# A graph layer with a routed expert layer on one core: another order for the first loads, for TensorE's last products of a step, and for GpSimd's tail

## The chip, the cores and the metric

The program runs on one core of a Trainium2 chip. The metric is the device time of one execution in microseconds. TensorE does matrix products and transposes, VectorE (DVE in the profile), ScalarE (ACT) and GpSimd (POOL) the rest, and SyncE (SP) issues most loads. Each engine runs its own list of instructions in order; they meet at semaphores.

## The reference

`x` has 32 x 256 tokens of 128 values, `adj` 32 matrices of 256 x 256.

```python
def gnn(x, adjacency, epsilon, W1, b1, rms_weight, W2, b2):
    agg = epsilon * x + einsum('bnm,bmd->bnd', adjacency, x)
    h = einsum('bnd,dh->bnh', agg, W1) + b1                  # 128 -> 512
    h = silu(h * rsqrt(mean(h * h) + 1e-6) * rms_weight)
    return einsum('bnh,hd->bnd', h, W2) + b2                 # 512 -> 128

def ffn(x, gamma, beta, Wr, br, W1, b1, W2, b2):
    xn = layernorm(x) * gamma + beta
    top2 = top_k(xn @ Wr + br, 2)                            # of 8 experts
    return sum over the two of softmax_share * (gelu(xn @ W1[e] + b1[e]) @ W2[e] + b2[e])

x = x + gnn(layernorm(x), adj, ...)
x = x + ffn(layernorm(x), ...)
```

## The kernel before

**First part.** The 8192 tokens are 16 groups of 512 (4 tiles of 128 tokens). `STEPS` is 19, and a step works on up to six groups at once, each at another stage: group s is loaded and normalised (`stats1`, `add_epsilon`, `normalise1`), group s-1 is aggregated over its neighbours (`aggregate`), group s-2 is widened to 512 (`widen`, `square`, `weigh`, `rms`), group s-3 gets its silu, is transposed and narrowed (`silu`, `turn_hidden`, `keep_turned`, `narrow`), group s-4 is added to its input, normalised, transposed and sent through the router (`residual`, `stats2`, `scale2`, `normalise2`, `turn_to_features`, `expert_input`, `router`), group s-5 gets its two experts, its shares and its places (`route`, `shares`, `choose`, `rank_pairs`, `places`), and the rows of group s-6 are stored into a table in DRAM (`rows_dram`), sorted by the pair of experts (`send_rows`, one indirect DMA of GpSimd for each tile). Each engine's order within a step is written out by hand.

**Second part.** There are 28 pairs of experts. The second part takes 92 tiles of 128 rows of one pair each: 20 tiles (`EARLY`) that are known to be full after group 11, 44 more, and 28 partly filled ones. For tile i SyncE loads the rows (`load_rows`, into a ring of `RING` = 16 buffers; from tile 16 on it waits until the result of the tile 16 before has been stored). TensorE's step i transposes tile i, multiplies tile i-2 with the two experts' first weights (`w1_low`, `w1_high`), and tile i-4 with the second weights. For the first 64 tiles the first weights are copied to a fixed place, since they are known only at run time: both halves by ScalarE in tiles 0 to 19, and from tile 20 on the high half of every even tile by GpSimd (`place_high`). ScalarE applies gelu, VectorE adds biases and shares and writes `result` (12 buffers), and GpSimd stores it (`send_result`, an indirect DMA). VectorE's `tail` does the rest of groups 14 and 15 between the first 15 tiles, and so do the lists of the other engines, since the rows of the last groups must be stored before tile 20 can be loaded.

**GpSimd's tail before** is a list by hand: the four sends of group 13 in two pairs around `scale2` and `put_tokens` of group 15, `shares` of group 14, four sends of group 14, three results, `shares` of group 15, three results, four sends of group 15, nine results (6 to 14), and then one result for each step.

**The start.** SyncE loads `x_tok` of group 0 and at once `adj` of group 0. ScalarE's queue loads the constants (`fixed`, 207 KB), `eps_col`, then `gw1_sb`, `gb1_row` and `rms_bc`, which share the semaphore `wide_in`. TensorE's list begins with `sum_weights`, which waits for all three, and only then comes `aggregate(0)`. `fold_gw1` on VectorE adds the sums to the weights, and `widen(0, 0)` waits for that.

## Time and profile before

| | |
|---|---|
| median of 3 runs | 462.79 us (462.18 to 462.91) |
| profiled execution, its own time | 462.02 us |
| its span, first to last instruction | 460.2 us |
| TensorE busy | 404.1 us (88%) |
| VectorE, ScalarE, GpSimd busy | 306.8, 280.3, 247.4 us |
| first part at a steady pace | 12.98 us a step |
| tile 20 to tile 91 in the second part | 1.9 to 3.3 us a tile |

A row of a timeline gives start and length in us, the engine, the line of the kernel, the operation with its tiles as out<-in, and in brackets how long the engine sat idle and what ended that. "issue" is time in which an engine waited for nothing that the profile shows, and "remote" (or "another core or an unknown queue") is a wait that the profile can put down to no finished instruction. PEclk is TensorE's granted clock, 1.0 being its higher level.

### The profile page before, as it was taken

Reading aid. Unit: us, or ns where it says so; the run is one execution under the profiler, and the core shown is the slowest. Engines: PE = TensorE matmul, PEld = TensorE weight load, DVE = VectorE, ACT = ScalarE, POOL = GpSimd, SP = SyncE. Lnnn points to the kernel's source line nnn. Section 1 sums busy time; section 2 is a strip of 40 time slices with the busy share of each in tenths; the row PEclk is TensorE's granted clock in tenths of the full one; section 3 lists DMA queues with packets and bytes.
Section 4 is the critical chain, followed back from the end, with each engine's and each line's share of the span. In section 5 each row is a group of like instructions: output and inputs, shape, how many; then the busy total and the mean of one; then the engine's idle time right before and its main releaser. Section 6 shows DMA issues by size and latency. Waiting matters only on the chain.

```text
span 460.2 us, 11870 instructions
## 1 busy us (share of the span) xinstructions
PE 404.1 (88%) x2894; PEld 346.2 (75%) x2894; DVE 306.8 (67%) x1303; ACT 280.3 (61%) x645; POOL 247.4 (54%) x315
## 2 busy tenths in 40 slices
PE   1999999999999999998739487999999999999970
PEld 0557877877777777776729486999999889999970
DVE  4596777889887777768544393666666766656540
ACT  1278776778777777787637253766666666444520
POOL 1123546676667777766642544465556555545450
PEclk9999999999999999999967887999999999999995
DMA  6679773223233221111253223555554433433110
GB/s 206 180 228 309 249 232 92 85 95 114 95 105 115 86 80 46 41 47 38 77 146 86 91 89 95 146 147 154 139 131 127 137 107 107 114 101 105 36 43 6
DMA packets 40890, 53.24 MB, mean 116 GB/s; under 512 B 5812, under 2 KB 35636, under 8 KB 40183
## 3 DMA queue, kind: packets, MB, share of 16 engines
q1 hardware_dynamic: 33040, 32.95, 25.9%
q0 software_dynamic: 6096, 18.52, 11.9%
q10 hardware_dynamic: 1686, 1.01, 0.8%
q8 instruction: 26, 0.43, 0.4%
q14 instruction: 42, 0.34, 0.3%
HBM read 37.75 MB, written 22.31 MB: 131 GB/s over the span
## 4 chain that ended last, share of the span: by engine, by line
PE 56%; DVE 11%; issue 10%; DVEq 9%; ACT 4%; another core or an unknown queue 3%; POOL 2%; DMA 2%; ACTq 0%; POOLq 0%
PE banks L576 10%; PE banks L599 9%; PE banks L737 9%; PE banks L724 9%; PE banks L564 6%; PE banks L585 5%; PE banks L621 3%; DVEq L1417 2%; DVEq L1434 2%; PE banks L611 2%; DVE acc L1417 2%; DMA rms_bc<-rms_w 2%; DVE result L1442 1%; DVEq L1442 1%
## 5 line engine op out<-in xcount | busy, mean ns | idle before, releaser
L526 POOL DMA_INDIRECT out<-result,rows_in x92 | 89.8, 976 | 81.9 <-DVE result L1442 68.1
L737 PE MATMUL banks<-w_sb,hidden_e 128*128 (+1 forms) x736 | 102.3, 283 | 4.8 <-DVE result L1442 2.5
L737 PEld LDWEIGHTS banks<-w_sb,hidden_e 128*128 128x128 f32 x736 | 92.5, 196 | 7.9 <-issue 7.3
L877 ACT ACTIVATE hidden_e<-banks 128x512 f32<-128x512 f32 x92 | 55.0, 598 | 56.3 <-PE banks L724 30.7
L489 POOL DMA_INDIRECT rows_dram<-rows_out,row_of x64 | 66.6, 1040 | 25.2 <-issue 14.7
L599 PE MATMUL banks<-gw_sb,hidden_t 128*128 128x128 f32 x512 | 68.8, 277 | 0.0
L576 PE MATMUL banks<-gw_sb,agg 128*128 128x512 f32 x128 | 66.3, 603 | 0.8 <-ACT agg L812 0.8
L599 PEld LDWEIGHTS banks<-gw_sb,hidden_t 128*128 128x128 f32 x512 | 63.5, 192 | 0.8
L1428 DVE SCALAR_TENSOR_TENSOR acc<-banks,rows_in,acc 128x128 f32<-128x128 f32 x92 | 32.2, 350 | 46.7 <-PE banks L737 25.0
L797 ACT ACTIVATE hidden<-hidden,rrms 128x512 f32<-128x512 f32 x64 | 45.7, 715 | 18.0 <-POOL rrms L466 18.0
L990 DVE TENSOR_TENSOR hidden<-banks,rms_bc 128x512 f32<-128x512 f32 x64 | 43.9, 687 | 12.2 <-ACT hidden L789 12.2
L871 ACT ACTIVATE xg_t<-banks,ones 128x128 f32<-128x128 f32 x92 | 33.5, 364 | 30.3 <-PE banks L706 14.6
L789 ACT ACTIVATE hidden<-banks 128x512 f32<-128x512 f32 x64 | 38.2, 597 | 22.0 <-PE banks L576 20.0
L585 PEld LDWEIGHTS banks<-fixed,hidden 128*128 128x128 f32 x256 | 30.1, 141 | 26.7 <-issue 22.3
L1417 DVE SCALAR_TENSOR_TENSOR acc<-b_bc,rows_in 128x128 f32<-128x128 f32 x92 | 33.4, 363 | 20.2 <-DVE result L1442 15.5
L724 PE MATMUL banks<-xg_t,w_low 128*128 128x128 f32 x256 | 41.9, 289 | 0.0
L724 PE MATMUL banks<-xg_t,w_high 128*128 128x128 f32 x256 | 41.3, 286 | 0.0
L585 PE MATMUL banks<-fixed,hidden 128*128 128x128 f32 x256 | 38.9, 275 | 2.7 <-ACT hidden_t L804 2.0
L706 PE MATMUL banks<-fixed,rows_in 128*128 128x128 f32 x92 | 26.4, 287 | 16.5 <-ACT xg_t L871 16.2
L804 ACT ACTIVATE hidden_t<-banks 128x512 f32<-128x512 f32 x64 | 37.8, 590 | 2.8 <-PE banks L585 2.6
L1434 DVE SCALAR_TENSOR_TENSOR acc<-b_bc,rows_in,acc 128x128 f32<-128x128 f32 x92 | 32.5, 353 | 10.1 <-issue 6.0
L453 POOL TENSOR_TENSOR rstd<-var,minus_half 128x4 f32<-128x4 f32 x16 | 16.6, 1039 | 41.5 <-DVE var L1017 41.5
(141 smaller groups left out, 708.1 us busy)
## 6 DMA issues: line engine op xcount, KB each, us to landing
rows_in<-rows_dram SPq DMA_DIRECT2D x92, 132.5 KB
adj<-adj_t SPq DMA_DIRECT2D x16, 512.0 KB, 3.9
x_tok<-x SPq DMA_DIRECT2D x16, 256.0 KB, 3.9
rows_dram<-idle_in POOLq DMA_DIRECT2D x1, 3710.0 KB
rows_dram<-idle_in SPq DMA_DIRECT2D x28, 132.5 KB
out<-result,rows_in POOLq DMA_INDIRECT x92
w_sb<-w SPq DMA_DIRECT2D x1, 1024.0 KB, 6.3
b_bc<-b SPq DMA_DIRECT2D x1, 1024.0 KB, 11.5
```

Source lines behind the costliest of these rows:

```text
L489: nc.gpsimd.indirect_dma_start(out=rows_dram, out_offset=bass.IndirectOffsetOnAxis(ap=row_of[:, g * TPG + t:g * TPG + t + 1], axis=0), in_ ...
L526: nc.gpsimd.indirect_dma_start(out=out, out_offset=bass.IndirectOffsetOnAxis(ap=rows_in[:, i % RING][:, IDX_AT:IDX_AT + 1].bitcast(U32), a ...
L576: pe.matmul(hid_ps[:, n % 3], agg[:, g % 2, t * P:(t + 1) * P], gw1_sb[:], start=True, stop=True).then_inc(hid_done, 1)
L585: last = pe.transpose(hidt_ps[:, c * P:(c + 1) * P], hidden[:, n % HR, c * P:(c + 1) * P], ident)
L599: last = pe.matmul(z_ps[:, t * P:(t + 1) * P], hidden_t[:, g % 2, c, t * P:(t + 1) * P], gw2_sb[:, c], start=False, stop=True, skip_group_ ...
L724: last = pe.matmul(h_ps(i)[:, w * HCE + c], w1_now[:, c * P:(c + 1) * P], xg_t[:, i % 4], start=True, stop=True)
L737: last = pe.matmul(y_ps(i)[:, w], hidden_e[:, i % 4, w * HCE + c], w2_sb[:, bass.ds(at + c * D, D)], start=(c == 0), stop=(c == HCE - 1))
L797: nc.scalar.activation(hidden[:, n % HR], hidden[:, n % HR], ACT.Silu, scale=rrms[:, g % 2, t:t + 1]).then_inc(silu_done, 1)
L877: nc.scalar.activation(hidden_e[:, i % 4], h_ps(i), ACT.Gelu).then_inc(gelu_done, 1)
L990: nc.vector.tensor_tensor(hidden[:, n % HR], hid_ps[:, n % 3], rms_bc[:], ALU.mult).then_inc(weighted, 1)
L1417: nc.vector.scalar_tensor_tensor(acc[:, i % AHEAD], b2_bc[:, bass.ds(expert(words, i, D, True), D)], rows[:, bass.ds(expert(words, i, 1, T ...
L1434: nc.vector.scalar_tensor_tensor(acc[:, i % AHEAD], b2_bc[:, bass.ds(expert(words, i, D, False), D)], rows[:, bass.ds(expert(words, i, 1, ...
```

## The change

- **First loads.** `fixed` is split: the identity (first 128 columns) is loaded first, the rest with the small loads. SyncE issues `adj` of group 0 only after `x_tok` of group 0 has landed, and ScalarE's queue waits for the same before `gw1` (now into `gw1_raw`, a slot of `hidden`), `gb1` spread over all partitions (`gb1_bc`, another slot) and `rms_bc`, with semaphores of their own.
- **The fold of gb1 into gw1.** `row_part` and its matrix product are gone. VectorE's `mix_gw1` makes gw1 + gb1/128 in step 0, `sum_weights` is one product of the raw weights and stands behind `aggregate(0)` in step 1, and `fold_gw1` moves to step 1. `prep_rank` moves to step 3.
- **Order within a step.** On TensorE `turn_to_features` moves behind `narrow(g3, 2)` and `router` behind `narrow(g3, 3)`; on ScalarE `keep_turned(g3, 3)` stands ahead of `expert_input(g4)`. On GpSimd `rms` works on two tiles at a time, twice a step, and the four sends of a group stand one by one between other work.
- **Second part.** `RING` is 20. GpSimd copies the high weights of all even tiles below 64, also of the first 20. Its tail is another list: the sends of rows and results stand between the copies, at most three or four in a row, results 0 to 3 in pairs. After the tail it is behind with the results (8 is the last sent), sends one result in each step from 20 to 22, and catches up in step 23.

```diff
-RING, SENDS = 16, 12
+RING, SENDS = 20, 12
...
         first_loads = [
-            (fixed[:], fixed_in), (eps_col[:], eps.partition_broadcast(P)),
-        ]
-        wide_loads = [
-            (gw1_sb[:], gw1), (gb1_row[:], gb1), (rms_bc[:], rms_w.partition_broadcast(P)),
+            (fixed[:, 0:P], fixed_in[:, 0:P]), (eps_col[:], eps.partition_broadcast(P)),
         ]
...
         def high_by_gpsimd(i):
-            return EARLY <= i < NT and i % 2 == 0
+            return i < NT and i % 2 == 0
...
+                if g == 0:
+                    sp.wait_ge(x_in[0], 16)
...
-            def rms(g):
-                pool.wait_ge(sumsq_ready, TPG * (g + 1))
+            def rms(g, half):
+                tiles = slice(2 * half, 2 * half + 2)
+                pool.wait_ge(sumsq_ready, TPG * g + 2 * half + 2)
...
                 if g6 is not None:
-                    send_rows(g6, (0,))
+                    send_rows(g6, 0)
+                if g4 is not None:
+                    put_tokens(g4)
+                if g6 is not None:
+                    send_rows(g6, 1)
                 if g4 is not None:
                     scale2(g4)
-                    put_tokens(g4)
...
-                    send_rows(g6, (1, 2, 3))
+                    send_rows(g6, 2)
                 if g2 is not None:
-                    rms(g2)
+                    rms(g2, 0)
+                if g6 is not None:
+                    send_rows(g6, 3)
+                if g2 is not None:
+                    rms(g2, 1)
...
-            send_rows(NG - 3, (0, 1))
+            send_rows(NG - 3, 0)
+            pool.wait_ge(table_ready, 2)
+            place_high(0)
+            send_rows(NG - 3, 1)
+            place_high(2)
+            send_rows(NG - 3, 2)
+            send_rows(NG - 3, 3)
             scale2(NG - 1)
             put_tokens(NG - 1)
-            send_rows(NG - 3, (2, 3))
             shares(NG - 2)
-            send_rows(NG - 2, (0, 1, 2, 3))
-            for i in range(3):
-                send_result(i)
-            shares(NG - 1)
-            for i in range(3, 6):
-                send_result(i)
-            send_rows(NG - 1, (0, 1, 2, 3))
-            for i in range(6, EARLY - SUM_LAG - 1):
-                send_result(i)
+            place_high(4)
+            send_rows(NG - 2, 0)
+            place_high(6)
+            send_rows(NG - 2, 1)
+            send_rows(NG - 2, 2)
+            send_rows(NG - 2, 3)
+            place_high(8)
+            send_result(0)
+            send_result(1)
+            shares(NG - 1)
+            place_high(10)
+            send_result(2)
+            send_result(3)
+            place_high(12)
+            send_rows(NG - 1, 0)
+            place_high(14)
+            send_rows(NG - 1, 1)
+            send_rows(NG - 1, 2)
+            place_high(16)
+            send_rows(NG - 1, 3)
+            send_result(4)
+            place_high(18)
+            sent = 5
+            for i in range(sent, sent + 4):
                 send_result(i)
+            sent += 4
             pool.wait_ge(table_ready, 4)
             for step in range(EARLY, TILES + SUM_LAG + 1):
-                if (i := tile_at(step, 0)) is not None and high_by_gpsimd(i):
-                    place_high(i)
-                if (i := tile_at(step, SUM_LAG + 1)) is not None:
-                    send_result(i)
+                if high_by_gpsimd(step):
+                    place_high(step)
+                while sent <= min(step - SUM_LAG - 1, TILES - 1):
+                    send_result(sent)
+                    sent += 1
+                    if step % 4 != 3 or sent > step - SUM_LAG - 1:
+                        break
...
             def sum_weights():
-                pe.wait_ge(wide_in, WIDE)
+                pe.wait_ge(gw1_in, 16)
                 pe.wait_ge(parts_made, 1)
-                pe.matmul(hid_ps[:, 2], minus_part[:], gw1_sb[:], start=True, stop=False)
-                pe.matmul(hid_ps[:, 2], row_part[:], gb1_row[:], start=False, stop=True).then_inc(sums_done, 1)
+                pe.matmul(hid_ps[:, 2], minus_part[:], gw1_raw, start=True, stop=True).then_inc(sums_done, 1)
...
-            sum_weights()
             pe.wait_ge(fixed_in_sbuf, 32)
...
                 if g1 is not None:
                     aggregate(g1)
+                if s == 1:
+                    sum_weights()
...
-                if g4 is not None:
-                    turn_to_features(g4)
                 if g3 is not None:
                     turn_hidden(g3, 3)
                     narrow(g3, 2)
                 if g4 is not None:
-                    router(g4)
+                    turn_to_features(g4)
                 if g3 is not None:
                     narrow(g3, 3)
+                if g4 is not None:
+                    router(g4)
...
+            act.wait_ge(x_in[0], 16)
+            act.dma_start(gw1_raw, gw1).then_inc(gw1_in, 16)
+            act.dma_start(gb1_bc, gb1.partition_broadcast(P)).then_inc(gb1_in, 16)
+            act.dma_start(rms_bc[:], rms_w.partition_broadcast(P)).then_inc(wide_in, 16)
...
+            def mix_gw1():
+                dve.wait_ge(gw1_in, 16)
+                dve.wait_ge(gb1_in, 16)
+                nc.vector.scalar_tensor_tensor(gw1_sb[:], gb1_bc, 1.0 / (D * SHIFT), gw1_raw, ALU.mult, ALU.add
+                                               ).then_inc(gw1_mixed, 1)
...
                 if s == 1:
-                    prep_rank()
+                    fold_gw1()
...
                 if s == 0:
-                    fold_gw1()
+                    mix_gw1()
```

## Rows read from the trace of the kernel before

**Rows 1.** The page: chain that ended last by engine.

```profile
PE 56%; DVE 11%; issue 10%; DVEq 9%; ACT 4%; another core or an unknown queue 3%; POOL 2%; DMA 2%; ACTq 0%; POOLq 0%
```

**Rows 2.** Windows of four stages: each engine's busy us (instructions), then clock, DMA share, GB/s.

```profile
0.00:14.28 14.28, 4.00 (x4) 1.00 (x4) 4.88 (x24) 1.49 (x2) 1.49 (x9) 1.00 0.74 220
...
131.36:196.25 64.89, 63.75 (x411) 49.04 (x411) 51.67 (x271) 50.00 (x110) 47.05 (x60) 1.00 0.25 78
...
229.71:286.45 56.74, 38.20 (x260) 36.13 (x261) 29.28 (x131) 26.99 (x70) 26.00 (x30) 0.77 0.37 103
286.45:366.84 80.39, 76.89 (x656) 74.81 (x656) 54.12 (x153) 53.97 (x136) 44.66 (x56) 0.99 0.52 140
```

**Rows 3.** Chain that ended last, first 20 us: start us, us, what.

```profile
2.73 7.50 DMA rms_bc<-rms_w
...
10.28 2.08 PE banks L644 x2
...
14.36 3.70 PE banks L564 x8
```

**Rows 4.** Timeline of VectorE, first 20 us (start us, us, engine, line, operation).

```profile
8.16 0.76 DVE L983 TENSOR_TENSOR adj<-adj,eps_ident 128x256 f32<-128x256 f32 x2
...
9.53 1.11 DVE L973 TENSOR_SCALAR xn<-x_tok,mv,rstd 128x128 f32<-128x128 f32 x4 [0.61 <-POOL rstd L446]
...
14.39 0.69 DVE L907 TENSOR_TENSOR gw_sb<-banks,gw_sb 128x512 f32<-128x512 f32 x1 [3.75 <-PE banks L645]
```

**Rows 5.** Line 397 in the first 20 us, last line of the answer.

```profile
DMA to landing us min/median/max: 3.8/5.6/6.9
```

**Rows 6.** Chain that ended last in one step of the first part, 157 to 171 us.

```profile
164.53 0.95 PE banks L576 x2
165.49 0.17 issue
165.65 0.66 PE banks L611 x4
...
167.64 0.79 PE banks L621 x8
168.43 0.99 PE banks L599 x8
169.43 0.86 PE banks L576 x2
```

**Rows 7.** Timeline of GpSimd: first and last sends of two runs.

```profile
226.11 1.06 POOL L489 DMA_INDIRECT rows_dram<-rows_out,row_of  x1 [0.18 <-issue]
...
231.28 0.96 POOL L489 DMA_INDIRECT rows_dram<-rows_out,row_of  x1 [0.30 <-issue]
...
250.65 1.04 POOL L489 DMA_INDIRECT rows_dram<-rows_out,row_of  x1 [7.49 <-DVE row_of L1097]
...
258.45 0.96 POOL L526 DMA_INDIRECT out<-result,rows_in  x1 [0.30 <-issue]
```

**Rows 8.** Waits between 229.71 and 286.45 us: total us, times, longest us.

```profile
DVE acc L1428 <- remote: 11.1, 2, 5.8
```

**Rows 9.** Timeline of VectorE, 225 to 300 us.

```profile
233.26 0.19 DVE L1030 TENSOR_TENSOR logits<-banks,br_bc 128x32 f32<-128x32 f32 x1 [5.49 <-remote]
...
250.09 0.35 DVE L1417 SCALAR_TENSOR_TENSOR acc<-b_bc,rows_in 128x128 f32<-128x128 f32 x1 [0.26 <-issue]
...
261.48 0.35 DVE L1428 SCALAR_TENSOR_TENSOR acc<-banks,rows_in,acc 128x128 f32<-128x128 f32 x1 [5.32 <-remote]
...
288.81 0.35 DVE L1417 SCALAR_TENSOR_TENSOR acc<-b_bc,rows_in 128x128 f32<-128x128 f32 x1 [0.65 <-DVE result L1442]
```

**Rows 10.** Line 522 on GpSimd, count and ns of one (min/median/max).

```profile
L522 POOL COPY w_high<-w_sb x22: 403/415/462, 296.0 to 384.9; 128x256 f32 x22
```

**Rows 11.** Line 1434 on VectorE, count and ns of one (min/median/max).

```profile
L1434 DVE SCALAR_TENSOR_TENSOR acc<-b_bc,rows_in,acc x92: 341/351/708, 235.4 to 440.8; 128x128 f32<-128x128 f32 x92
```

**Rows 12.** Timeline of TensorE: the transpose of tile 26.

```profile
306.58 0.27 PE L706 MATMUL banks<-fixed,rows_in 128*128 128x128 f32 x1
```

More of the change, by code:

```diff
@@ L209, in build @@
         hidden = sb("hidden", [P, HR, H1])
+        gw1_raw, gb1_bc = hidden[:, HR - 1], hidden[:, HR - 2]
         hidden_t = sb("hidden_t", [P, 2, HC1, GT])
@@ L457, in scale2 @@
                                         ).then_inc(rstd2_ready, 1)
[L459 to L461 removed]
+            def rms(g, half):
+                tiles = slice(2 * half, 2 * half + 2)
+                pool.wait_ge(sumsq_ready, TPG * g + 2 * half + 2)
+                if g >= 2 and half == 0:
                     pool.wait_ge(silu_done, TPG * (g - 1))
[L463 removed]
+                nc.gpsimd.tensor_tensor(meansq[:, tiles], sumsq[:, g % 2, tiles], rms_eps[:, tiles], ALU.add
                                         ).then_inc(meansq_ready, 1)
[L465 to L466 removed]
+                pool.wait_ge(meansq_ready, 2 * g + half + 1)
+                nc.gpsimd.tensor_tensor(rrms[:, g % 2, tiles], meansq[:, tiles], minus_half[:, tiles], ALU.pow
                                         ).then_inc(rrms_ready, 1)
@@ L481, in shares, with send_rows @@
                 nc.gpsimd.tensor_tensor(power[:], euler[:], apart[:], ALU.pow).then_inc(power_ready, 1)
-            def send_rows(g, tiles):
-                if 0 in tiles:
+            def send_rows(g, t):
+                if t == 0:
                     pool.wait_ge(shares_put, g + 1)
@@ L487, in send_rows @@
                     pool.wait_ge(rows_ready, g + 1)
-                for t in tiles:
-                    nc.gpsimd.indirect_dma_start(
-                        out=rows_dram,
-                        out_offset=bass.IndirectOffsetOnAxis(ap=row_of[:, g * TPG + t:g * TPG + t + 1], axis=0),
-                        in_=rows_out[:, g % RO, t], in_offset=None
-                    ).then_inc(rows_sent[g % RO], 16)
+                nc.gpsimd.indirect_dma_start(
+                    out=rows_dram,
+                    out_offset=bass.IndirectOffsetOnAxis(ap=row_of[:, g * TPG + t:g * TPG + t + 1], axis=0),
+                    in_=rows_out[:, g % RO, t], in_offset=None
+                ).then_inc(rows_sent[g % RO], 16)
             for s in range(STEPS):
@@ L847, in _ @@
                     square(g2, 3)
+                if g3 is not None:
+                    keep_turned(g3, 3)
                 if g4 is not None:
                     expert_input(g4)
-                if g3 is not None:
-                    keep_turned(g3, 3)
             words = {}
```

36 lines of the change are left out of this document (19 added, 17 removed).

## Prediction

> **What bounds the kernel now.** I read the chain that ended last first: TensorE has 56% of it, VectorE 11%, "issue" 10%, an unknown queue 3% [rows 1]. Then the windows by stage [rows 2]. From 131 to 196 us TensorE is busy 63.75 of 64.89 us: five steps of 12.98 us, the engine's own list sets the time. From 229.71 to 286.45 us it is busy only 38.20 of 56.74 us at a mean clock of 0.77, and that stage makes tiles 0 to 15, which at 1.9 us each would need 30. From 286 to 367 us it has 76.89 of 80.39 us, but VectorE's loop holds every fourth tile back a little. So there are three places: the start, the order within a step, and the 57 us between the two parts.
>
> **The start.** Before, TensorE waits for rms_bc until 10.28 us, then needs 4.1 us for two products, and group 0's aggregation begins at 14.36 [rows 3], although its inputs are ready when VectorE's normalisation of 9.53 + 1.11 ends at 10.64 [rows 4]. Now the aggregation goes first. But adj of group 0 leaves only when x has landed. An adj load takes 3.8 to 6.9 us [rows 5]; x landed before the statistics began, so I put the issue at 4.5 us and with 5 us under way (other loads run beside it) the landing at 9.5. Before, adj was in by 8.16 [rows 4]. Then add_epsilon 0.84 and normalisation 1.15: 11.5. Aggregation 3.7 us [rows 3] to 15.25, sum_weights 2.1 to 17.3, fold_gw1 0.7 [rows 4] to 18.0, and behind it on VectorE add_epsilon and normalisation of group 1 to 20.0, for which aggregate(1) waits. Before, aggregate(1) began at 19.9. The 3.7 us won in front of the first aggregation are lost behind it, since the fold now stands in VectorE's list ahead of group 1. I take 0; if adj lands at 8.3, it is 1.5 less; if the clock, which is still at its lower level of 1.2 GHz in these products (2.08 us for what takes 0.86 later [rows 3, 6]), stays there one product of 3.7 us longer, it is 2 more.
>
> **The order within a step.** In a step of before the products from widen(3) to the next widen(0) last from 164.53 to 169.43, 4.90 us: widen 0.95, a wait of 0.17 and 0.66 for turn_to_features, which comes just when ScalarE's second normalise2 ends, then 0.44, 0.89, router 0.79, narrow 0.99 [rows 6]. In the new order turn_to_features comes 1.3 us later and doesn't wait: 0.95 + 0.44 + 0.89 + 0.44 + 0.89 + 0.79 = 4.40. The 0.1 us that a product pays behind the router's small ones (0.99 for 0.89) moves to widen(0), so 4.49, and 0.41 us less a step. The cover: keep_turned(3) must end before narrow(3) and expert_input before the router; square, its read-out and keep_turned end 0.6 + 0.2 + 0.6 us behind widen(3), and narrow(3) starts 1.8 behind it, 0.4 to spare; expert_input ends 0.65 behind turn_to_features, and the router starts 0.9 behind it, 0.25 to spare. GpSimd gets a second pair of rms instructions, 1.3 us a step. Its list then sums to four sends 5.1, two rms pairs 2.7, scale2 1.3, scale1 1.1, shares 1.5 and put_tokens 0.2, 11.9 us of a step of 12.57, so it fits, and what would be late first is normalise2, with 1 us to spare. Nine steps (4 to 6, 11 to 16) at 0.41 make 3.7. In the four steps with a fold of expert weights VectorE's chain leads until rank_pairs, and only 0.06 is saved each: 0.2. The last steps 0.3. Sum 4.2 us less.
>
> **Between the two parts.** Here the rows say something odd. At 255.9 us ScalarE and VectorE stop; VectorE goes on at 261.48 after 5.32 us of "remote" [rows 9]. What they wait for is TensorE's signal that a product is finished, and its products were started long before. It happens three times, and each time GpSimd is at the end of a run of sends: five from 226.11 to 231.28, VectorE waits until 233.26; seven from 250.65 to 258.45 (1.30 us from one to the next), a wait of 5.32; and seven more later, a wait of 5.8 [rows 7 to 9]. The last two are the 11.1 us of L1428 [rows 8]. In the first part three sends in a row do no harm. I read it thus: while GpSimd sends without a break, TensorE's signals are held back, and they come about 1 us after the last send. What holds them I can't see.
>
> The change breaks the runs. First hold: after three sends come a wait and a copy, so the router's signal of 230.0 us should arrive at 230.4 in place of 233.26; two more sends then delay scale2 by 0.5. Gain 2.3 us. The other holds: VectorE begins tile 5 at 250.09 and tile 16 at 288.81 [rows 9] (the first and the last of 12 starts), 38.7 us for 11 steps. The same 12 starts with the waits for held signals taken out give 1.65 + 2.4 + 2.8 + 2.4 + 2.2 + 2.6 + 2.8 + 3.1 + 2.6 + 1.9 + 2.5 = 27.0. Gain 11.7 us, if no new hold comes.
>
> Now GpSimd's list. A copy costs 0.42 us [rows 10], with its gaps 0.7. It waits for the last row numbers of group 14 until 250.65 before [rows 7], so until about 248.3. From there to the copy for tile 24 stand 27 sends (35.1 us), 10 copies (7), 3 reads of the word (1.5) and shares (1.4): 45 us, it is ready at 293.3. TensorE takes tile 24's first product in step 26, before at 306.58 [rows 12], less 2.3 and 11.7 at 292.6. GpSimd, hidden before, is just on the path. And its list ends with results 11 to 18 in a row, eight sends with nothing between them, since step 23 catches up: the same shape as the runs that held TensorE for 5 us. VectorE can hide little of that, for it sets the pace there. I take 5.0 us for this run (between 0 and the 7.5 that a hold of before cost with the slow products behind it) and 1.5 for the shorter runs of two to four. The copies taken from ScalarE (0.4 us each) gain nothing: it is busy 26.99 of 56.74 us here [rows 2]. RING 20 frees SyncE's loads of tiles 16 to 19, which no tile waited for: 0.
>
> From tile 16 on the pace is VectorE's, as before. An op of VectorE took 0.708 us in place of 0.351 when it met a GpSimd copy, once in 92 [rows 11]; with 22 copies before and 32 now that is 0.2 us more, left out. The Trainium skill, page "SBUF — State Buffer", section "SBUF: two separate sides", speaks against the copies: an op of VectorE with two SBUF inputs and a GpSimd op that reads SBUF lock each other out for a whole instruction. If each of the ten new copies did so it would be 3.6 us; the trace has it once in 22 copies.
>
> **Sum.** 462.0 (the profiled execution's own time) + 0 - 4.2 - 2.3 - 11.7 + 6.5 = 450.3. The median of the runs is 0.8 above that execution, so 451.
>
> **Rivals.**
> - A: no new hold. For it: single sends and pairs between copies do little harm, and GpSimd may still wait for results in its run of eight. Then 6.5 less: 444.5. Chance 0.22.
> - B: breaking the runs doesn't help, a copy of 0.4 us isn't break enough, and the holds cost what they did. For it: a hold ended about 1 us after the last send, and a copy's gap is 0.7. Only the step's order counts: 462.8 - 4.2 = 458.6. Chance 0.14, with 0.03 of it within 0.2% of before, where the start loses its 2 us too and the steps gain half.
> - C, slower: GpSimd becomes the bound of the tiles. Each copy stands in line with sends, and TensorE waits for it. It is 45 us of work with 0.7 us to spare at tile 24; to eat all the gains it must be 13 us later, that is when each of the 10 copies costs 1.3 us more than 0.7, by a late signal that it waits for itself. Then 464 to 468. Chance 0.08.
> - D: the port lock as in the rule above, in a kernel that otherwise does as forecast: each of ten copies costs VectorE 0.357 us more [rows 11]: 454.6. Chance 0.06. Against it: the one case in 22.
>
> Forecast itself 0.50. The range goes from 442 (A with 1.5 us won at the start and 1 for the first hold gone whole) to 460 (B with most of the start's loss), which leaves out C and the edge of A and B, under 0.2. One measurement tells 0.2% (0.9 us) from no change. Faster 0.89, same 0.03, slower 0.08.
>
> **What would show it.** First aggregation at 11.5 us and aggregate(1) still near 20. Steps of 12.57 us in place of 12.98, turn_to_features without a wait. The router's last signal of the first part reaching VectorE within 0.5 us. No "remote" of over 2 us until GpSimd's run of results 11 to 18, and one of about 5 us in it. Tile 16 on VectorE 14 us earlier than before, less the steps' part. If "remote" stays over 15 us in all, B is right; if GpSimd shows no idle time from the first copy to tile 24 and TensorE waits for w_high, C.

## The result and the profile after

The changed kernel took 460.64 us (median of 19 runs, 458.54 to 462.47) beside 463.31 us for the kernel before (19 runs in turn with it, 461.9 to 465.6): ratio 0.992, 95% interval [0.990, 0.994]. The forecast was 451 and its range 442 to 460; the direction was right, the size some four times too large. The profiled execution took 459.9 us, its span is 458.0.

The page's chain that ended last, by engine: TensorE has a larger share than before [rows 1], and the unknown queue did not shrink.

```profile
PE 63%; DVE 10%; issue 9%; DVEq 6%; another core or an unknown queue 4%; DMA 2%; POOL 1%; ACT 1%; ACTq 0%; POOLq 0%
```

Windows of the changed kernel, the same stretches as in [rows 2] from the second on (busy us of TensorE, its weight loads, VectorE, ScalarE, GpSimd, with instructions; then clock, DMA share, GB/s):

```profile
131.36:196.25 64.89, 64.59 (x424) 51.33 (x425) 52.07 (x274) 51.01 (x114) 52.01 (x73) 1.00 0.25 76
```
```profile
229.71:286.45 56.74, 43.72 (x327) 41.50 (x328) 35.88 (x148) 29.84 (x75) 26.76 (x35) 0.84 0.35 98
286.45:366.84 80.39, 72.42 (x600) 70.14 (x599) 49.96 (x142) 48.79 (x124) 45.18 (x56) 0.96 0.50 135
```

In the first part TensorE does 13 instructions more in the same 64.89 us. In the second window it does 327 in place of 260, so the stage between the parts is better filled. But in the third it does 600 in place of 656, and is busy 72.42 of 80.39 us in place of 76.89: work is lost where little was lost before.

Chain that ended last, first 20 us (start us, us, what). The aggregation starts at 10.62 and not at 14.36 [rows 3]:

```profile
4.16 4.48 DMA adj<-adj_t
...
10.62 3.75 PE banks L603 x8
14.37 1.49 PE banks L683 x2
...
17.24 1.04 DVE xn L1022 x4
...
18.32 1.78 PE banks L603 x7
```

The same chain in a plain step. The transposes L650 follow the products L638 without a wait, and the next widen (L615) follows the router (L660):

```profile
163.09 0.44 PE banks L650 x4
163.53 0.89 PE banks L638 x8
164.42 0.85 PE banks L660 x8
165.27 0.96 PE banks L615 x2
...
177.07 0.85 PE banks L660 x8
```

From router to router are 12.65 us. Now the stage between the parts. GpSimd's timeline, then VectorE's, in brackets how long the engine sat idle and what ended it:

```profile
220.98 1.06 POOL L493 DMA_INDIRECT rows_dram<-rows_out,row_of  x1 [0.18 <-issue]
...
225.15 0.97 POOL L493 DMA_INDIRECT rows_dram<-rows_out,row_of  x1 [0.17 <-issue]
226.13 0.41 POOL L533 COPY w_high<-w_sb 128x256 f32 x1
...
227.98 0.96 POOL L493 DMA_INDIRECT rows_dram<-rows_out,row_of  x1 [0.30 <-issue]
...
287.34 0.97 POOL L537 DMA_INDIRECT out<-result,rows_in  x1 [0.29 <-issue]
...
293.67 0.96 POOL L537 DMA_INDIRECT out<-result,rows_in  x1 [0.30 <-issue]
```
```profile
229.84 0.19 DVE L1079 TENSOR_TENSOR logits<-banks,br_bc 128x32 f32<-128x32 f32 x1 [7.19 <-remote]
...
245.48 0.35 DVE L1467 SCALAR_TENSOR_TENSOR acc<-b_bc,rows_in 128x128 f32<-128x128 f32 x1 [0.26 <-issue]
...
254.27 0.35 DVE L1478 SCALAR_TENSOR_TENSOR acc<-banks,rows_in,acc 128x128 f32<-128x128 f32 x1 [3.56 <-remote]
...
276.80 0.35 DVE L1467 SCALAR_TENSOR_TENSOR acc<-b_bc,rows_in 128x128 f32<-128x128 f32 x1 [0.65 <-DVE result L1492]
...
294.28 0.35 DVE L1478 SCALAR_TENSOR_TENSOR acc<-banks,rows_in,acc 128x128 f32<-128x128 f32 x1 [3.48 <-remote]
```

I call a wait put down to "remote" while GpSimd sends a *hold*. The first hold is longer than before (7.19 us, before 5.49 [rows 9]), although copies stand between its sends. Not all of it is a signal that comes late: ScalarE's `expert_input` had itself been held (3.03 us, until 226.01), so the router's products ran only from 226.66 to 228.16, and VectorE went on 1.7 us after their end. Tile 5 to tile 16 on VectorE takes 31.3 us in place of 38.7. Then comes the run of results 11 to 16, and a hold in it: the transpose of 291.57 us had ended at 291.84, and ScalarE read it at 294.69, when the sixth send had just ended (294.63). The waits between 220 and 300 us (total us, times, longest):

```profile
ACT xg_t L912 <- remote: 12.0, 3, 5.4
...
DVE logits L1079 <- remote: 7.2, 1, 7.2
DVE acc L1478 <- remote: 7.0, 2, 3.6
...
POOL w_high L533 <- PE banks L763: 5.7, 4, 2.1
```

TensorE's transposes of tiles 3, 16 and 24 in the changed kernel (before: 241.75, 286.45 and 302.71 in the same view):

```profile
238.01 0.45 PE L745 MATMUL banks<-fixed,rows_in 128*128 128x128 f32 x1 [4.46 <-ACT xg_t L912]
...
273.41 0.27 PE L745 MATMUL banks<-fixed,rows_in 128*128 128x128 f32 x1
...
299.21 0.42 PE L745 MATMUL banks<-fixed,rows_in 128*128 128x128 f32 x1
```

So 3.7 us are won up to tile 3 and 9.3 more up to tile 16, 9.5 are lost again between tiles 16 and 24, and 1.3 behind them; that leaves the 2.2 us by which the span is shorter.

### The profile page after: what moved, and what is told of

Same layout as the page of the kernel before. It is cut to its first block, busy times and chain, and to the rows that moved or that the text cites. A ratio compares the mean times of both kernels' runs of the same rounds, so it can differ in the third digit from the quotient of the medians.

```text
span 458.0 us, 11932 instructions
## 1 busy us (share of the span) xinstructions
PE 401.1 (88%) x2892; PEld 347.5 (76%) x2892; DVE 307.4 (67%) x1303; ACT 277.0 (60%) x635; POOL 264.2 (58%) x357
## 4 chain that ended last, share of the span: by engine, by line
PE 63%; DVE 10%; issue 9%; DVEq 6%; another core or an unknown queue 4%; DMA 2%; POOL 1%; ACT 1%; ACTq 0%; POOLq 0%
PE banks L776 11%; PE banks L763 11%; PE banks L615 11%; PE banks L638 10%; PE banks L603 7%; PE banks L624 5%; PE banks L660 3%; DVEq L1467 2%; DVEq L1484 2%; PE banks L650 2%; PE banks L745 1%; DVE acc L1467 1%; DVE result L1492 1%; DVEq L1478 1%
## 5 line engine op out<-in xcount | busy, mean ns | idle before, releaser
L493 POOL DMA_INDIRECT rows_dram<-rows_out,row_of x64 | 65.9, 1030 | 23.6 <-issue 11.7
L615 PE MATMUL banks<-gw_sb,agg 128*128 128x512 f32 x128 | 67.3, 611 | 0.9 <-DVE gw_sb L954 0.9
L638 PE MATMUL banks<-gw_sb,hidden_t 128*128 128x128 f32 x512 | 67.6, 275 | 0.0
L638 PEld LDWEIGHTS banks<-gw_sb,hidden_t 128*128 128x128 f32 x512 | 63.5, 192 | 0.8
L1478 DVE SCALAR_TENSOR_TENSOR acc<-banks,rows_in,acc 128x128 f32<-128x128 f32 x92 | 32.2, 350 | 44.7 <-PE banks L776 26.2
L830 ACT ACTIVATE hidden<-banks 128x512 f32<-128x512 f32 x64 | 38.2, 597 | 30.5 <-PE banks L615 25.8
L624 PEld LDWEIGHTS banks<-fixed,hidden 128*128 128x128 f32 x256 | 30.5, 141 | 34.4 <-issue 29.7
L603 PE MATMUL banks<-adj,xn 128*128 128x256 f32 x128 | 32.3, 398 | 11.6 <-DVE xn L1022 11.6
L603 PEld LDWEIGHTS banks<-adj,xn 128*128 128x128 f32 x128 | 25.2, 199 | 22.3 <-issue 16.8
```

Of the source, the lines that this page charges most:

```text
L493: nc.gpsimd.indirect_dma_start(out=rows_dram, out_offset=bass.IndirectOffsetOnAxis(ap=row_of[:, g * TPG + t:g * TPG + t + 1], axis=0), in_ ...
L603: last = pe.matmul(agg_ps[:, b * NODES:(b + 1) * NODES], xn1[:, g % 2, 2 * b + c], adj[:, g % AR, 2 * b + c], start=(c == 0), stop=(c == 1))
L615: pe.matmul(hid_ps[:, n % 3], agg[:, g % 2, t * P:(t + 1) * P], gw1_sb[:], start=True, stop=True).then_inc(hid_done, 1)
L624: last = pe.transpose(hidt_ps[:, c * P:(c + 1) * P], hidden[:, n % HR, c * P:(c + 1) * P], ident)
L638: last = pe.matmul(z_ps[:, t * P:(t + 1) * P], hidden_t[:, g % 2, c, t * P:(t + 1) * P], gw2_sb[:, c], start=False, stop=True, skip_group_ ...
```

## The experiments

Each run is compared with the kernel before in the same set of runs; a set runs on one chip, one kernel after the other.

**Set 1: the change in parts.** Four kernels: the start and the step's order together; GpSimd's tail and the copies alone; the step's order alone; and the whole change with a loop from tile 20 on that sends at most two results in a step:

```diff
-                while sent <= min(step - SUM_LAG - 1, TILES - 1):
-                    send_result(sent)
-                    sent += 1
-                    if step % 4 != 3 or sent > step - SUM_LAG - 1:
-                        break
+                for _ in range(2 if step % 4 == 3 else 1):
+                    if sent <= min(step - SUM_LAG - 1, TILES - 1):
+                        send_result(sent)
+                        sent += 1
```

The kernel with the start and the step's order is the changed one with its second part undone; the two others undo other parts of it (the second part alone keeps `RING` at 16). Some of the lines of the first:

```diff
-RING, SENDS = 20, 12
+RING, SENDS = 16, 12
...
-            return i < NT and i % 2 == 0
+            return EARLY <= i < NT and i % 2 == 0
...
-            pool.wait_ge(table_ready, 2)
-            place_high(0)
             send_rows(NG - 3, 1)
-            place_high(2)
```

> The changed start and the changed order of a step, with the GpSimd tail, the copies and RING of before. Theory S (the second part of the program lost time by its new list): the first part's 5.1 us (last rank step on VectorE 208.4 -> 203.3 in the two profiles) survive, and the kernel is 4.5 to 5.1 us faster than before, so 458, and faster than the whole change by about 2. Theory N (the second part is a queue of stores with a fixed length; what is won ahead of it is waited away): within 1 us of before.

> Kernel of before with only the new GpSimd tail and the copies of tiles 0 to 19 on GpSimd (RING stays 16, since RING 20 needs the memory that the new start frees). Theory S: 2 to 3 us slower than before (465.5). Theory N: 3 to 4 us faster, since the whole change is and the first part brings nothing. My prediction's terms would give 7.5 us faster.

> Kernel of before with only the new order of a step (TensorE, ScalarE, the two halves of rms and the split sends of GpSimd). Theory S: nine plain steps at 0.33 us, the fold steps at 0, the last ones 0.3 to 0.5: 3.4 us faster, and the start's 1.6 is missing against the run with both. If the start's gain were eaten by the steps behind it, this run would equal that with both.

> The whole change, but GpSimd sends at most two results in a step from tile 20 on (the run of results 11 to 18 in step 23 is gone, GpSimd catches up by one result every four steps). Theory H (TensorE's signals are held while GpSimd sends without break): the hold that ends at 294.6 us (ScalarE 5.43, TensorE 4.61 us of waiting) goes, and tile 24 starts 4 to 7 us earlier; of that 3 to 5 us reach the end. Rival Q (the wait there is for GpSimd's copy of tile 24's weights, that is for the length of its list and not for the run): the same, since the list up to the copy of tile 24 is 4 sends shorter: 5 us too, but the holds of results 5 to 10 stay in both. Rival V (VectorE sets the pace from tile 16 on and takes the loss back): under 1 us.

| set 1 | median us | ratio, 95% interval |
|---|---|---|
| before | 448.19 (20 runs) | |
| start and step's order | 441.50 | 0.983 [0.980, 0.987] |
| second part alone | 448.34 | 1.000 [0.998, 1.002] |
| step's order alone | 445.65 | 0.993 [0.991, 0.995] |
| whole, two results at most | 440.65 | 0.984 [0.981, 0.988] |

The surprise is the first row: the kernel before takes 448 us here, not 463. And no wait put down to "remote" stands among those between 200 and 330 us of any of the four. The second part alone brings nothing: theory S's loss of 2 to 3 us is not here, nor the gain of 3 to 4 that theory N gave it. S's 458 for the first part isn't here either, since the whole level has moved. The first part brings 6.7 us, more than the 4.5 to 5.1 that I expected of it, and the order within a step alone 2.5, less than 3.4. What the list with at most two results does to a hold could not be seen, for there was none.

**Set 2: is it the chip?**

> The kernel before once more, for a profile on the chip of these experiments. On the chip of the four runs ahead it took 448.2 us, not 462.8, and its variants there show no wait for a held signal. Theory C (the holds belong to the chip that ran the first comparison, not to the kernel alone): where this kernel takes 448, its trace shows no remote wait of over 1 us in the stretch 226 to 300 us, and tile 16 on VectorE comes about 12 us earlier than the 288.8 us of the first trace; where it takes 463, the three holds are there. Rival L (the 14.6 us are spread, a generally faster chip): every stage is 3% shorter, the steps of the first part too.

> The whole change once more beside before. Theory C: without holds the second part's change is worth nothing (it was 1.000 alone), so the ratio is that of the first part, 0.983 to 0.987 and about 441.5; with holds it is 0.992 as in the first comparison. Theory S as I put it first (the new list itself loses 3 us on any chip): 444.

The third kernel gives the copies of tiles 0 to 19 back to ScalarE and leaves GpSimd's waits where they were:

```diff
-            return i < NT and i % 2 == 0
+            return EARLY <= i < NT and i % 2 == 0
...
-                nc.gpsimd.tensor_copy(w1_high[:, i % 4], w1_sb[:, bass.ds(at, HE)]).then_inc(high_placed2, 1)
+                if i >= EARLY:
+                    nc.gpsimd.tensor_copy(w1_high[:, i % 4], w1_sb[:, bass.ds(at, HE)]).then_inc(high_placed2, 1)
```

> The whole change, but ScalarE makes all copies of tiles 0 to 19 again; GpSimd's sends keep their new order and the waits that the ten copies had. Theory K (a copy of 0.4 us is neither a break for the signals nor a cost): within 1 us of the whole change, with or without holds. Rival P (GpSimd's copies come late and delay TensorE, or lock VectorE out): 2 to 3 us faster than the whole change.

The fourth replaces the list by hand with one send a tile:

```diff
+            plan = rows_of(NG - 3) + [None] + rows_of(NG - 2) + results(0, 2) + rows_of(NG - 1) + results(2, 7)
+            for step in range(EARLY):
+                if high_by_gpsimd(step):
+                    place_high(step)
+                elif step >= 4:
+                    pool.wait_ge(h_done, step - 3)
+                if plan[step] is not None:
+                    plan[step][0](*plan[step][1])
...
+                for _ in range(2 if step % 4 == 3 and step > 24 else 1):
```

> The whole change, but from tile 0 to tile 24 GpSimd makes one send a tile, each released by the progress of TensorE's tiles (wait for h_done of four tiles earlier), and then one send more every fourth tile. A gap of 0.5 us or more stands between most sends. Theory H (holds come from unbroken sending): on a chip with holds none over 1 us remains there and the time falls by 8 to 12 us against the whole change; on a chip without holds it is within 1 us of it. Rival G (it is the number of sends in flight or the events on that chip, not the unbroken run): on a chip with holds they stay.

| set 2 | median us | ratio, 95% interval |
|---|---|---|
| before | 447.82 (its profiled run 448.51) | |
| whole change | 442.16 | 0.987 [0.984, 0.990] |
| copies on ScalarE | 442.26 | 0.986 [0.983, 0.989] |
| one send a tile | 441.16 | 0.984 [0.981, 0.986] |

Again no holds, on another chip. Theory C holds against theory L, a generally faster chip: the last aggregation of the kernel before starts at 196.63 us here and at 196.09 in the first trace, and tile 24 to tile 64 take 84 us in both. Only the stretch between differs. VectorE's timeline of the kernel before, to be held against [rows 9]; the second line is its start of tile 5, the third of tile 16:

```profile
230.67 0.19 DVE L1030 TENSOR_TENSOR logits<-banks,br_bc 128x32 f32<-128x32 f32 x1 [2.43 <-PE banks L621]
...
247.52 0.35 DVE L1417 SCALAR_TENSOR_TENSOR acc<-b_bc,rows_in 128x128 f32<-128x128 f32 x1 [0.26 <-issue]
...
275.89 0.35 DVE L1417 SCALAR_TENSOR_TENSOR acc<-b_bc,rows_in 128x128 f32<-128x128 f32 x1 [0.65 <-DVE result L1442]
```

The changed kernel in this set, GpSimd's first list and the router's result on VectorE:

```profile
221.03 1.06 POOL L493 DMA_INDIRECT rows_dram<-rows_out,row_of  x1 [0.18 <-issue]
...
228.04 0.96 POOL L493 DMA_INDIRECT rows_dram<-rows_out,row_of  x1 [0.30 <-issue]
```
```profile
225.51 0.19 DVE L1079 TENSOR_TENSOR logits<-banks,br_bc 128x32 f32<-128x32 f32 x1 [2.81 <-PE banks L660]
```

The sends are the same as in the first trace to 0.1 us (221.03 to 228.04, there 220.98 to 227.98), and VectorE goes on at 225.51 in the middle of them, not at 229.84 behind the last. Six sends with two copies between them hold nothing here. So the list of sends alone doesn't make a hold; a condition that isn't in the kernel has to be there too. The copies, on GpSimd or on ScalarE, make no difference here (442.2 and 442.3); a set with holds was not run with them on ScalarE.

**Set 3: four of them on one chip.**

> The whole change, beside the three others of this call on one chip. Two chips have now run the kernel before in 448 us without a hold, the first comparison's chip in 463 with three. On a chip without holds: 0.983 to 0.990 of before. With holds: 0.992 again, and holds of 3 to 7 us in the trace.

> Only the new start and the new order of a step. Without holds: level with the whole change within 1.5 us (the whole one spares a stretch of 3.4 us at the low clock near 262 us, 1.6 us in its profile). With holds, theory S (the new list makes the holds longer): 3 to 4 us faster than the whole change; rival M (the holds would grow anyway when the first part ends earlier): equal to it.

> One send a tile up to tile 24, released by the tiles' progress. Without holds: as the whole change within 1 us. With holds, theory H (unbroken sending holds the signals): 8 to 12 us faster than the whole change; rival G (the sends themselves, however spaced): as the whole change.

> The whole change without the run of results 11 to 18. Without holds: 0 to 1 us faster than the whole change (the profile of its first run started tile 24 at 281.8 in place of 282.2 us). With holds, theory H: 3 to 7 us faster than the whole change; rival G: level with it.

| set 3 | median us | ratio, 95% interval |
|---|---|---|
| before | 465.01 | |
| whole change | 461.11 | 0.993 [0.990, 0.995] |
| start and step's order | 456.23 | 0.983 [0.981, 0.986] |
| one send a tile | 456.55 | 0.985 [0.982, 0.987] |
| whole, two results at most | 461.40 | 0.994 [0.991, 0.996] |

The holds are back, and this is the chip of set 1, which ran the kernel before in 448: so theory C's word "chip" was wrong, it is the set of runs. This set is the one that answers the first question. With holds, the new list of the second part costs 4.9 us against the first part alone (461.1 and 456.2, intervals apart): theory S, not M. One send a tile gives that back, 4.6 us, but not the 8 to 12 that theory H promised nor the nothing of theory G, and two at most gives nothing (461.4). Its profiled run, of 457.1 us, was the fastest of its ten, so its trace shows it better than it is.

The first part alone shows what became of the first hold. With holds, in set 4 below, its list sends four rows without a break and then waits for VectorE. GpSimd's first and last of the four, and VectorE's logits:

```profile
219.87 1.06 POOL L493 DMA_INDIRECT rows_dram<-rows_out,row_of  x1 [0.18 <-issue]
...
223.76 0.96 POOL L493 DMA_INDIRECT rows_dram<-rows_out,row_of  x1 [0.30 <-issue]
```
```profile
225.84 0.19 DVE L1055 TENSOR_TENSOR logits<-banks,br_bc 128x32 f32<-128x32 f32 x1 [4.31 <-PE banks L636]
```

The wait ends with the router's products, and it ends at 225.84, against 225.58 in set 1 without holds. The changed list puts two copies and two more sends in front of `scale2` and ends its run at 228.94; there VectorE goes on at 229.84. All three traces of that list with holds have this wait of 7.2 us for "remote", and none of the six others of the new order with holds has one.

**Set 4: pace and runs.** The paced version waits for the tiles' progress before every send and makes up its lag slowly. The two others change the first part alone, from tile 20 on:

The paced version, against the one with one send a tile:

```diff
+                elif step <= TILES:
+                    pool.wait_ge(h_done, step - 3)
-                for _ in range(2 if step % 4 == 3 and step > 24 else 1):
+                for _ in range(2 if step % 8 == 7 and step > 24 else 1):
```

Pairs (for fours, `% 4 == 3`):

```diff
-                if (i := tile_at(step, SUM_LAG + 1)) is not None:
-                    send_result(i)
+                if step % 2 == 1 or step == TILES + SUM_LAG:
+                    while sent <= step - SUM_LAG - 1:
+                        send_result(sent)
+                        sent += 1
```

> One send a tile over the whole second part, every one released by the progress of the tiles, and the lag of nine results given back by one send more in every eighth tile. In the set with holds the version without this pacing behind tile 24 took 92.3 us from tile 24 to 64 where the first part alone took 85.0, with sends two and three in a row. Theory H (unbroken sending): with holds these 40 tiles take 84 to 87 us, and the kernel 449 to 453, 3 to 6 us under the first part alone. Rival G (number of sends, however spaced): 90 us or more for the 40 tiles. Without holds: level with the first part alone, within 1.5 us.

> The first part alone, but from tile 20 on GpSimd sends the results in pairs, every second tile. Theory H, with holds: a tile in two pays 0.3 to 0.9 us, 10 to 30 us in all at most, at least 3. Rival G: no difference, for the sends are as many. Without holds: no difference.

> As the one with pairs, but four results in a row every fourth tile: a run of 5.2 us, some 17 of them. Theory H, with holds: each run holds the products' signals for 2 to 4 us, of which 1 to 3 reach the tiles: 20 to 50 us slower than the first part alone. Rival G: no difference, and without holds none over 2 us (the last results leave together).

> The first part alone again, the measure for the three others: 0.983 of before under either condition, as in both sets so far.

| set 4 | median us | ratio, 95% interval |
|---|---|---|
| before | 464.31 | |
| paced | 455.10 | 0.982 [0.979, 0.984] |
| pairs | 455.76 | 0.982 [0.979, 0.985] |
| fours | 456.33 | 0.985 [0.982, 0.988] |
| start and step's order | 455.11 | 0.982 [0.979, 0.984] |

With holds again. Pairs and fours tell nothing, for the edit did not do what I wanted. GpSimd's timeline of the one with fours:

```profile
314.77 0.97 POOL L537 DMA_INDIRECT out<-result,rows_in  x1 [0.16 <-issue]
317.32 1.09 POOL L537 DMA_INDIRECT out<-result,rows_in  x1 [1.58 <-DVE result L1471]
319.44 0.96 POOL L537 DMA_INDIRECT out<-result,rows_in  x1 [1.03 <-DVE result L1471]
```

GpSimd is ahead of the tiles, so each send still waits for its own result. A list has no clock: an instruction that stands behind another is not later unless something makes it wait.

The paced version is worth a look, though its time is level with the first part alone. TensorE's transposes of tiles 16, 24 and 64, first in the first part alone, then paced:

```profile
278.66 0.42 PE L721 MATMUL banks<-fixed,rows_in 128*128 128x128 f32 x1
...
294.88 0.27 PE L721 MATMUL banks<-fixed,rows_in 128*128 128x128 f32 x1
...
380.22 0.27 PE L721 MATMUL banks<-fixed,rows_in 128*128 128x128 f32 x1
```
```profile
271.15 0.30 PE L733 MATMUL banks<-fixed,rows_in 128*128 128x128 f32 x1 [1.09 <-ACT xg_t L900]
...
288.56 0.27 PE L733 MATMUL banks<-fixed,rows_in 128*128 128x128 f32 x1
...
380.31 0.27 PE L733 MATMUL banks<-fixed,rows_in 128*128 128x128 f32 x1
```

It is 6.3 us ahead at tile 24 and 0.1 us behind at tile 64: 91.8 us for these 40 tiles, where theory H gave 84 to 87 and theory G 90 or more. Pacing did break up the holds between 229 and 290 us (the longest remote wait on any engine is 1.9 us, in the first part alone 6.2), but between 290 and 380 us, where the first part alone has none, it has 16.4 us of them on three engines. They don't go away, they come later.

**Set 5: real runs, and a late lag.**

Real fours, on the first part alone, and the late lag, on the paced version:

```diff
+                if step % 4 == 3 and step < TILES + SUM_LAG:
+                    pool.wait_ge(result_ready, step - SUM_LAG)
+                    for i in range(step - SUM_LAG - 4, step - SUM_LAG):
+                        send_result(i)
```
```diff
+                pool.wait_ge(result_ready, min(step - SUM_LAG, TILES))
+                for _ in range(2 if step >= NT + 2 and step % 3 == 0 else 1):
```

> The first part alone, but from tile 20 on GpSimd waits for the last of four results and then sends the four in a row, 19 runs of 5.2 us. With holds (before at 462 to 465), theory H (an unbroken run holds TensorE's signals until its end): each run costs the tiles 1 to 3 us, 20 to 50 us in all. Theory E (a send costs only where it covers a signal that is due, at most its own length, and the steady tiles have slack): 0 to 10 us. Without holds (before at 448): under 3 us, for a copy that comes late behind a run, in either theory.

> One send a tile as in the paced version up to tile 20, then every send right behind the result of a tile, with the lag of eight results kept up to tile 64 and made up behind it, one send more in every third tile. With holds: tile 24 at 288 to 289 us, tiles 24 to 64 in 85 us as with the first part alone, and the end 4 to 6 us earlier than with the first part alone, 0.970 to 0.974 of before, if the sends that are made up are what cost 6.4 us there. If the lag itself costs (loads and buffers), 0.982 again. Without holds: 0.983 to 0.987.

| set 5 | median us | ratio, 95% interval |
|---|---|---|
| before | 449.02 | |
| real fours | 450.14 | 1.003 [1.001, 1.005] |
| late lag | 441.19 | 0.983 [0.980, 0.986] |

No holds in this set, so neither question got its answer. The fours are real here (317.19, 318.46, 319.73 and 321.00 us), no signal is held in them, and still they cost some 8.6 us against the first part alone (441.5 in set 1, at the same level of the kernel before). Their traces put 5.3 us of that between tiles 24 and 64 (88.9 us for 83.6), where the copies stand behind them, and 3.1 behind tile 64 (76.2 for 73.1), where there are no copies and the last results leave together. The waits between 306 and 370 us:

```profile
PEld banks L743 <- POOL w_high L533: 8.2, 7, 1.5
...
PE banks L743 <- POOL w_high L533: 6.9, 7, 1.3
```

Seven waits, 6.9 us. My bound of 3 us for all of it was too low. The late lag is level with the other good versions without holds; with holds it wasn't tried.

**All stages side by side.** Worked out from TensorE's transposes of tiles 3, 16, 24 and 64 in each trace, us:

| | to tile 3 | 3 to 16 | 16 to 24 | 24 to 64 | 64 to end |
|---|---|---|---|---|---|
| with holds: before | 241.8 | 44.7 | 16.3 | 84.4 | 73.1 |
| changed, first comparison | 238.0 | 35.4 | 25.8 | 85.7 | 73.1 |
| changed, set 3 | 237.5 | 38.3 | 24.8 | 85.7 | 73.1 |
| start and order, set 4 | 234.3 | 44.4 | 16.2 | 85.3 | 73.1 |
| one send a tile, set 3 | 234.2 | 36.4 | 17.9 | 92.3 | 73.4 |
| two at most, set 3 | 237.8 | 35.1 | 20.6 | 88.5 | 73.1 |
| paced, set 4 | 234.5 | 36.6 | 17.4 | 91.8 | 73.1 |
| without: before, set 2 | 239.2 | 34.4 | 16.3 | 83.8 | 73.1 |
| changed, set 2 | 233.7 | 32.4 | 16.2 | 83.7 | 73.1 |
| start and order, set 1 | 234.1 | 33.7 | 16.2 | 83.6 | 73.1 |

Tile 3 to tile 64 takes 144 to 149 us in all ten traces with holds, however the sends lie, and 132 to 135 in nine of the ten without (136.9 with real fours). Kernel for kernel the difference is 11 us (before) to 17 (the changed kernel in set 3), and none of the lists took it away: it is mostly moved.

## Why the prediction was wrong

The step that failed is the claim that the change breaks the runs: that copies of 0.4 us between sends let TensorE's signals through, so that both hold terms, -2.3 and -11.7, could be taken whole. With holds the changed list kept a first hold of 7.2 us and three more of 3.4 to 5.4. The terms of the sum, in its own order, against the first comparison:

- **The start: 0, measured 1.5.** The second aggregation starts at 18.32 us, before at 19.79. adj landed at 8.64 (4.16 + 4.48) and not at 9.5, since x had landed at 4.14: the end that I named as "1.5 less" came true. The clock stayed low for one aggregation only (3.75 us, the next takes 1.99), so the 2 us more at the other end did not come. Medians put the start higher (445.65 without it, 441.50 with it, 4.2 us), the last aggregation of the two traces lower (192.36 and 191.50, 0.9 us). It is worth 1 to 4 us; the runs don't settle it closer.
- **The order within a step: the mechanism right, each step a little short.** 12.65 us in place of 12.98, not 12.57: 0.33 for 0.41 a step, mostly because the router takes 0.85 there and not 0.79. The wait in front of turn_to_features is gone. The first part ends some 5 us earlier with the start's 1.5 in it; forecast 4.2 with none. By itself the order brings 2.5 us (445.65 for 448.19).
- **Hold 1: forecast -2.3, and it grew.** To tile 3 the kernel won 3.7 us, where the first part alone wins 7.4 (241.8 and 234.3, from two sets). A copy of 0.4 us between sends does not let the signals through. The new order with its old tail, which stops after four sends, has no hold there at all (225.84 us); the six sends of the new tail brought it back (229.84). The description of the change as "three or four in a row" did not count that.
- **The other holds: forecast -11.7, measured -7.4.** The 27.0 us that I worked out for VectorE's 12 starts if nothing is held is a good figure: without holds the changed kernel takes 27.1 (241.29 to 268.41) and the kernel before 28.4. With holds it took 31.3. So the list without holds was priced well; that the changed list is one without holds was the error.
- **The new run of results: forecast +6.5, measured 9.5 from tile 16 to 24 and 1.3 behind it.** The place and the mechanism were right: ScalarE waits 5.43 us for a remote signal in it, and tile 24 comes at 299.2, not at 292.6. The size was short by 4.3; a hold of 3.44 us at results 5 to 8, which I had priced within 1.5 us, fits most of that. GpSimd's copies (5.7 us of waiting for TensorE's products) were late by TensorE, and nowhere in this trace does TensorE wait for a copy, so rival C is out. (Its "0.7 us to spare" was a slip: by my own sum the copy came 0.7 us after TensorE's need, 293.3 and 292.6.)
- **The rivals.** A is out, for there is a new hold. B, at 458.6 and with 0.14, was nearest, and right that a copy isn't break enough. That its price comes within 2 us is in part luck: the holds did not stay as they were, tiles 3 to 16 took 9.3 us less and what follows 10.8 us more. The holds are no property of the list alone: in ten of the twenty traces, over three of six comparisons, they are not there, and the kernel before takes 448 us. A price taken from one trace held a condition of that set of runs. D's 3.6 us are not there: ten copies more or fewer on GpSimd make no difference without holds (442.2, 442.3). Single VectorE operations do stretch when they meet a copy (0.55 us at 247.12 and 256.61 in place of 0.35), more often than the once that I had: of 27 bias operations (`acc<-b_bc,rows_in`, with or without `acc`) that overlap a copy in the changed kernel's trace, 7 take 0.42 to 0.61 us.

The Trainium skill's rule of the port lock (page "SBUF — State Buffer", section "SBUF: two separate sides") says that such an operation and the copy lock each other out for a whole instruction. The changed kernel's trace agrees in kind: in the 7 cases the copy begins first or within 0.05 us, and where VectorE is clearly first the copy is the longer one (0.44 to 0.53 us for 0.40) and VectorE keeps its 0.35. But the seven stretches sum to 1.2 us over all 32 copies, and no run shows a cost of the ten new ones above its noise of about 1 us.

What is shown: the change's first part is worth 0.983 under either condition (0.983, 0.983, 0.982), its second part 1.000 without holds and a loss of 4.9 us with them. The changed kernel in the first comparison fits the sum of the two: 0.983 of 463.3 and 4.9 make 460.3, measured 460.6. That copies between the sends don't end a hold is shown in three traces. That the sends hold the signals is argued from their times, though versions whose sends are spaced have only short waits (2.6 us at most up to tile 64). What is not settled: which condition turns the holds on, and why most of their cost stays when the sends are moved.

No version beats the start and the step's order alone under both conditions. Without holds the whole change with two results at most is level with it (440.65 and 441.50), with holds it is 5 us slower. The version to keep is the first part alone.

## What to carry to other kernels

Before a wait of unknown origin is made the main term of a forecast, look whether it is there in a second set of runs: here 14 to 17 of the kernel's 463 us came and went with the set (448 to 449 us without), and the change's effect with it. Edits whose gain lies in the engine's own list (an instruction moved behind a wait) kept their value under both conditions, those that played with the unexplained wait did not. Where sends stand in one list with copies that another engine needs, send one by one: one send a tile is level with the first part alone under both conditions (0.984 and 0.985 of before), where the changed list costs 4.9 us with holds, also with two at most, and real fours some 8.6 without any hold. Without holds a single run of six to eight costs about 1 us at most (442.2 us, and 441.2 with one a tile).

## What the runs showed of the hardware

- **Holds that aren't in the program.** In three sets ScalarE and VectorE wait 3 to 7 us for "remote" while GpSimd issues indirect DMAs, up to 4 us after the product that they wait for has ended (before, 257.13 and 261.48 us). All 40 such waits of 3 us and more in these traces end behind four to seven sends less than 0.7 us apart (with or without copies between them), from 0.5 us before to 2.3 us after the end of the latest; the two traces with one send a tile have none. The same 1.0 us sends, 1.3 us apart, hold nothing in three other sets, one of them on the same chip.
- **Four sends and a stop hold less than six.** With holds, VectorE's wait at the end of the first part ends with the router's products when the run is four sends, and 0.9 us after the last send when it is six with two copies between them.
- **The traces differ too.** In all ten traces with holds the pages give no time to landing for the sends of results; in seven of the ten without, they give 2.4 to 2.6 us.
- **The clock falls behind a gap.** In the changed kernel TensorE is busy 2.31 us of the 5 in which its run of results holds it, and the granted clock of the next 5 us is 0.54 in place of 1.00, most of them at the lower level:

```profile
290.00:295.00 5.00, 2.31 (x19) 1.97 (x17) 0.84 (x3) 0.31 (x1) 3.72 (x4) 1.00 0.36 107
295.00:300.00 5.00, 2.66 (x12) 2.66 (x13) 2.73 (x8) 2.64 (x8) 1.59 (x2) 0.54 0.35 91
```

  Over the stretch between the parts the mean granted clock is 0.77 before [rows 2] and 0.84 in the changed kernel; in the changed kernel of set 2, without holds, 0.93:

```profile
229.71:286.45 56.74, 48.04 (x411) 47.04 (x412) 39.96 (x153) 36.51 (x92) 35.20 (x45) 0.93 0.45 126
```

- **A GpSimd copy of 0.4 us** does not break a hold (7.2 us in three traces with two copies between the sends). Moved from ScalarE, ten of them cost nothing that runs without holds can tell (442.2 and 442.3 us).
